# Scatters and gathers of a state-space kernel on GpSimd: the waits for their landing moved to the end of a pair

## The reference

```python
xz = silu(in_proj_w @ x + in_proj_b)              # 768 rows: x_ssm, res, gate
xf = silu(depthwise_conv3(x_ssm) + dw_b)          # 256 rows, along the tokens
perm = argsort(mobius_score)                      # one order of the 1024 tokens per head (2 heads)
dbc = dbc_w @ xf + dbc_b                          # per head: dt, 8 of B, 8 of C
x_h, dt, B_t, C_t = (take(v, perm) for v in (xf, softplus(dt), B, C))
y_h = selective_scan(x_h, dt, -exp(A_log), B_t, C_t, D)
y = take(y_h, argsort(perm))                      # back to the order of the image
out = x + silu(out_proj_w @ (y * silu(gate) + res) + out_proj_b)
```

## Time and profile before

| what | value |
|---|---|
| median of 3 runs | 946.37 us (946.17 to 948.2) |
| the profiled execution | 940.44 us, span of its instructions 938.6 us |
| busy: PE, VectorE, ScalarE, GpSimd | 84%, 62%, 60%, 37% of the span |
| the chain that ended last, by engine | PE 58%, ACT 13%, POOL 8%, DVE 7%, issue 7%, DMA 6% |
| scatters L396 | 128, mean 1353 ns, 339.0 us of GpSimd's idle time before them |
| gathers L410 | 128, mean 1040 ns, 139.3 us of idle time before them |
| PE, residuals and projects L1192 | 768, mean 597 ns, 4.2 us of idle time before them |

### The profile page before, as it was taken

How to read it: one execution, slowest core, us unless ns; L and a number is a source line. 1 busy time by engine, 2 the same in 40 slices (tenths; PEclk the granted TensorE clock), 3 DMA queues, 4 the chain that set the end, 5 groups by cost and what they waited for, 6 DMA issues and landing times.

```text
span 938.6 us, 10961 instructions
## 1 busy us (share of the span) xinstructions
PE 790.8 (84%) x3732; PEld 508.5 (54%) x3732; DVE 580.3 (62%) x1112; ACT 563.7 (60%) x1069; POOL 344.3 (37%) x292
## 2 busy tenths in 40 slices
PE   1104888568999999999999999999999999977896
PEld 0003554466456745684568456755765566644753
DVE  6884614483759456864777476837692769267824
ACT  4850648343776486648754785578567756653452
POOL 0001224066504850385028621862086307530150
PEclk9655898688999999999999999999999999989899
DMA  8920005914785476637673759373937292757132
GB/s 304 412 84 0 1 32 146 121 51 147 191 108 205 152 194 81 221 121 219 81 225 129 207 83 232 128 209 74 234 129 209 73 159 87 213 127 142 55 126 90
DMA packets 109816, 136.10 MB, mean 145 GB/s; under 512 B 40761, under 2 KB 90434, under 8 KB 109762
## 3 DMA queue, kind: packets, MB, share of 16 engines
q1 hardware_dynamic: 97474, 99.61, 43.2%
q0 software_dynamic: 12288, 35.80, 11.6%
HBM read 82.83 MB, written 53.61 MB: 145 GB/s over the span
## 4 chain that ended last, share of the span: by engine, by line
PE 58%; ACT 13%; POOL 8%; DVE 7%; issue 7%; DMA 6%; SPq 2%; POOLq 0%; DVEq 0%; ACTq 0%
PE pj L1192 25%; PE pj L1314 7%; ACT big L522 5%; PE st L1234 5%; PE pj L1255 5%; POOL xt_scratch L396 4%; PE tp L1209 4%; PE tp L1211 3%; POOL crow L410 3%; PE pj L1265 3%; ACT xf L505 2%; DMA crow<-cd_scratch 2%; ACT L522 2%; DMA crow<-yt_scratch,idx 2%; PE tp L1304 2%
## 5 line engine op out<-in xcount | busy, mean ns | idle before, releaser
L1192 PE MATMUL pj<-xb,inw 128*128 128x512 f32 x768 | 339.7, 597 | 4.2 <-POOL xb L378 4.2
L396 POOL DMA_INDIRECT xt_scratch<-stage,idx x128 | 173.2, 1353 | 339.0 <-issue 267.3
L1192 PEld LDWEIGHTS pj<-xb,inw 128*128 128x128 f32 x768 | 143.3, 191 | 171.4 <-issue 163.7
L410 POOL DMA_INDIRECT crow<-yt_scratch,idx x128 | 133.2, 1040 | 139.3 <-DMA yt_scratch<-rs 57.7
L902 DVE SCALAR_TENSOR_TENSOR xf<-xs,small,xf 128x1024 f32<-128x1024 f32 x64 | 81.6, 1284 | 131.5 <-ACT xf L498 130.3
L1314 PE MATMUL pj<-gt,outw 128*128 128x512 f32 x256 | 118.1, 593 | 0.6 <-DVE gt L1056 0.6
L1255 PE MATMUL pj<-xp,mblk 128*128 128x128 f32 x512 | 72.7, 287 | 23.2 <-ACT gt L572 15.7
L545 ACT COPY ch<-tp 128x256 f32<-128x256 f32 x128 | 42.8, 381 | 82.2 <-PE tp L1246 82.0
L1255 PEld LDWEIGHTS pj<-xp,mblk 128*128 128x128 f32 x512 | 65.8, 201 | 29.4 <-ACT gt L572 21.5
L534 ACT COPY stage<-tp 128x256 f32<-128x256 f32 x128 | 47.9, 374 | 55.0 <-PE tp L1211 52.3
L1062 DVE SCALAR_TENSOR_TENSOR xb<-xb,pcur,rs 128x1024 f32<-128x1024 f32 x32 | 41.0, 1284 | 60.3 <-ACT rs L603 60.3
(11 more groups left out here) (191 smaller groups left out, 1138.9 us busy)
## 6 DMA issues: line engine op xcount, KB each, us to landing
xb<-in_x SPq DMA_DIRECT2D x26, 1024.0 KB, 8.7
xp<-xt_scratch SPq DMA_DIRECT2D x8, 2048.0 KB, 11.9
crow<-cd_scratch SPq DMA_DIRECT2D x64, 256.0 KB, 12.5
yt_scratch<-rs SPq DMA_DIRECT2D x16, 1024.0 KB, 4.9
out<-xb SPq DMA_DIRECT2D x16, 1024.0 KB, 7.4
xp<-xt_scratch SPq DMA_DIRECT2D x8, 272.0 KB, 8.7
xt_scratch<-stage,idx POOLq DMA_INDIRECT x128
crow<-yt_scratch,idx POOLq DMA_INDIRECT x128, 2.8
```

The lines of the kernel that those rows point to most:

```text
L396: pool.indirect_dma_start(out=xt_d.ap(), out_offset=bass.IndirectOffsetOnAxis(ap=idx[:, k:k + 1], axis=0), in_=v(stage, (nt * H + h) * ROW ...
L410: pool.indirect_dma_start(out=v(crow, k * NB * P, (1, NB * P)), out_offset=None, in_=yt_d.ap()[0:(h + 1) * N], in_offset=bass.IndirectOffs ...
L1192: last = nc.tensor.matmul(o[:, :], v(inw, ct * 3 * C + col + ot * P, (1, P)), x_view(par, b, ct, nt * HALF, HALF), start=(ct == 0), stop=( ...
```

## The change

GpSimd's cycle `i` becomes: the scatters of pair `i + 1`, the scaling of x, the gather of head 0, the gather of head 1, then the holds for the landing of the gather of head 0, of head 1, and of the scatters. The waits ahead of each gather for its stored y, and for `w_ready`, stay. The scatters of pair 0, ahead of the first cycle, keep their wait. Nothing else is edited.

```diff
                         in_offset=bass.IndirectOffsetOnAxis(ap=idx[:, k:k + 1], axis=0)).then_inc(y_gathered[h], 16)
-                hold(y_gathered[h], 128 * (i + 1))
+                if h == H - 1:
+                    hold(y_gathered[0], 128 * (i + 1))
+                    hold(y_gathered[1], 128 * (i + 1))
 
             def cycle(i):
                 if i < PH - 1:
                     scatter(i + 1)
                 if i < PH - 2:
                     scale_x(i + 2)
+                for h in range(H):
+                    gather(i, h)
                 if i < PH - 1:
                     scattered(i + 1)
-                for h in range(H):
-                    gather(i, h)
```

## The result

The changed kernel takes 949.08 us (median of 7 runs, 947.12 to 951.91) against 945.61 us for the kernel before on the same chip (7 runs, 944.59 to 948.2). The ratio is 1.0039, 95% interval 1.002 to 1.0058: slower by some 3.5 us, where 6.4 us less had been forecast. The profiled run took 947.81 us (span 946.0 us, 938.6 before).

A forecast was written before the change was run, and what follows sets the result against it. The chain of waits was taken to lie mostly on PE, with gathers a small part, binding in pairs 6 and 7. The sum 0 + 5.8 + 0.6 = 6.4 us took the median 946.37 to 940.0, range 938.2 to 944.3.

The forecast's parts named there:

- Pair 6, the first wait: First gather of pair 6 starts at 803.7 instead of 805.97; nobody needs this, as PE does not wait there.
- D: Rival: GpSimd's issues beside VectorE's convolution taps slow them in pairs 0 to 5, giving 962.8 us; chance 0.05.
- Pairs 0 to 5: Second gather moves some 5.2 us forward, but PE's own work covers it and nothing waits: 0 us gained.
- Pair 6, the second wait: Second gather starts 5.1 us earlier; PE's wait falls from 5.89 to 1.3 us and its clock rises: 5.8 us gained.
- costs nothing: Pair 6: VectorE is done draining the first head's tiles at 827.5, so this adds no time.
- Pair 7, 0.6 us: Only 0.75 us of the second gather's 4.46 us wait can be had; 0.6 us gained.
- Carrying over the 5.9 us: Runs' median lies 5.9 us above the profiled 940.44 us; this difference is added unchanged to the forecast.
- C: Rival: GpSimd stands inside the issue instead of at the semaphore, so each wait is paid elsewhere: 946.4 us; chance 0.07.

The follow-up runs named there:

- s_only: The kernel before with only the wait for the scatters' landing moved behind the gathers; the wait between the gathers stays: 951.42 us, ratio 1.0032.
- g_only: The kernel before with only the waits for the gathers' landing moved to the end of the pair; the scatters' wait stays: 953.59 us, ratio 1.0056.
- b0: The kernel before, unedited, run and profiled again: 947.47 us, ratio 1.0000.
- b_shift: The kernel before with 104 already fulfilled waits added on TensorE, to move its instruction fetches in the program: 947.90 us, ratio 0.9975.
- a_late: The changed kernel with each pair's first gather held until ScalarE has copied head 1's last result: 949.40 us, ratio 0.9986 to the kernel before.
- a_shift: The changed kernel with 104 already fulfilled waits added on TensorE, to move its instruction fetches: 955.15 us, ratio 1.0059 to the kernel before.
- b_late: The kernel before with each pair's first gather held until ScalarE has copied head 1's last result: 953.31 us, ratio 1.0075.
- a0: The changed kernel, unedited, run and profiled again: 956.16 us, ratio 1.0089 to the kernel before.
- the two plain ones: The changed kernel and the kernel before, each with its indirect gathers replaced by plain transfers of the same size: 934.95 and 935.30 us, ratios 0.9874 and 0.9870.
- b_single: The kernel before with one gather in flight at a time for head 0 of pair 7: 960.85 us, ratio 1.0145.

## Why the prediction was wrong

The step that failed is "Pair 6, the first wait": "Nobody needs this: PE reaches the first head's transposes with no wait now." It asked who waits for the first gather, and not what the gather does to the work beside which it now runs. That wait cost GpSimd 2.55 us and kept the gather behind the turns of head 1. Without it eight indirect transfers are in flight beside turns 12 to 15 and the last results, TensorE's counts are held for up to 7.5 us (806.92 to 814.41), and the second y store, on which the next step rests, comes 7.9 us later after the first than in the profile before. s_only shows it alone (21.4 between the stores), g_only, b0 and b_shift show it absent, a_late takes it away again. None of the rivals had it. D came nearest, as the one in which GpSimd's work slows another engine, but looked at the wrong one.

- Pairs 0 to 5, 0 us: right within 1 us in the first two profiles (485.7 against 484.7 us), and b0 has 485.7 too. That PE's order covers the moved gathers holds there, but not always: g_only has 489.7 and a_shift 488.2, with late counts in pair 3 of both (up to 2.5 us) and in pair 5 of g_only (1.4 us).
- Pair 6, the second wait, 5.8 us: not gained. The rest of pair 6 fell by as much, 42.1 to 36.3 us, but that is a coincidence of size: it falls by 7.0 in s_only, which keeps this wait. Behind a store that is 7.7 us late the wait no longer binds, and the rest is shorter because it is counted from the late store. Where the store is in time, taking the wait away gave nothing in g_only (42.3 in both): PE then waits 5.91 us for VectorE to drain the first head's tiles, of which the prediction says that it "costs nothing". With the gathers behind the turns it gave 4.6 us (b_late and a_late). So the sum's largest term rests on a store in time and on a VectorE that drains in time, and the change itself upsets the first. Of the smaller terms, the gather started 5.5 us behind the store instead of 6.4, PE waited 1.89 us instead of 1.3, and the clock behind it was 0.79 and not 1.00.
- Pair 7, 0.6 us: not there. Its stores were 18.0 us apart instead of 13.0, and the rest was 1.2 us longer. The 5.0 us are no effect of the change, since b0 has them too.
- The sum over the two profiles, 7.4 us: up to the first store of pair 6 −1.0, stores of pair 6 +7.9, rest of it −5.8 (the two together +2.0), the way to pair 7 +0.1, stores of pair 7 +5.0, rest of it +1.2. Without the 5.0 it is 2.4, of the size of the 3.5 us between the medians. The 8.7 us between the medians of b0 and a0 are more than pair 6 explains (57.5 against 56.0), and the one profile of each does not place the rest: 3.8 us of their difference lie ahead of pair 1's first y store, which comes anywhere from 307.6 to 315.7 us in the fourteen profiles.
- Carrying over the 5.9 us between the profiled execution and the median as if it had nothing to do with the change: wrong as well. b0's profile, 949.15 us, has the late counts in pairs 3 and 7 that the first one lacks, so part of the 5.9 us is a cost of the kind on which the change acts. How many of the timed runs pay it, no profile tells.
- C fell: issues kept their pace of 1.25 us with two sets of eight behind each other (pair 6 of g_only). D fell: the convolution taps keep their median, against the earlier trace rows, and the longest of them grew by 0.05 us:

```profile
L904 DVE SCALAR_TENSOR_TENSOR xf<-xs,small,xf x64: 1276/1284/1336, 101.1 to 730.4; 128x1024 f32<-128x1024 f32 x64
```

How sure is the cause? Take, from 240 us on, the instructions of ScalarE and VectorE that use a tile of TensorE (all but the segment and chunk sums of the scan) and before which their engine stood idle for over 0.15 us, and count the delay of each from the end of its matmul, or from when its engine became free if that was later. The profiles with indirect gathers (the changed kernel's and those of the ten experiments other than the two plain ones) hold 2200 of them. Of 1313 with no packet of GpSimd's queue within 0.6 us, none was more than 0.6 us late; of 887 with one, 87. Together with b_single, the plain kernels and the late ones, this shows that in this kernel it takes several indirect transfers close behind each other. They are not sufficient: the first profile has 79 such instructions beside them and none late, and pairs 1, 2 and 4 hardly ever have one.

What holds the counts is open. The Trainium skill ("Perfetto Trace Analysis", "Tensor Engine Instruction (MATMUL, LD_WEIGHTS)") says that a matmul's end in a profile is an estimate, and that its semaphore is raised only when PSUM has acknowledged the last bytes and is seen elsewhere after a further step. That agrees with a late count behind a matmul that the trace ends in time; whether the acknowledgement or the way of the count is slow, no run here shows. Nor was it tried how it goes with two in flight.

## What to carry to other kernels

A wait that nobody needs for its data may keep two things apart: before it is removed, look at what will then run side by side, on the consumers of every engine that signals there, not only at who waits for the moved transfer. When the profiled execution is quicker than all timed runs, find out what it was spared before its rows become the terms of a sum. And when an idle engine starts long after its producer's recorded end, compare the recorded semaphore counts: a burst of them, closer together than the work that raised them, is a held signal and not a slow engine.

## What the runs showed that was not expected

TensorE's counts to ScalarE and VectorE were held while several indirect transfers of GpSimd were in flight, then came in bursts 0.06 us apart, the longest holds at the last landing of a set of eight or up to 1.3 us after it: 814.41 with the landing at 814.42 (changed kernel, pair 6), 901.70 with 901.63 (b0, pair 7), 832.01 with 831.53 (g_only, pair 6), 837.41 with 836.16 (a_late, pair 6). Shorter ones ended while transfers were still in flight (808.74 in the changed kernel, pair 6). Plain transfers of the same bytes on the same queue held none in these places, and made the kernel 1.3% faster (0.9870, with the rows of y unsorted), so the indirect gathers cost this kernel some 12 us in all: their slower issue, their scattered rows and the held signals together.
